# Graph attention on one Trainium2 core: P turned by VectorE blocks and transfers inside SBUF instead of by TensorE

## The chip, the core and the metric

The kernel runs on one core of a Trainium2 chip. The metric is the device time of one execution in microseconds (us). TensorE is the engine of the matrix products (PE in the rows, PEld its weight loads), VectorE is DVE, ScalarE is ACT, GpSimd is POOL, and SyncE, whose queue issues the DMAs here, is SP.

## The reference, cut to what matters

`x` is 2048x256, `adj` 2048x2048 (sparse, with many exact zeros), the projections `Wq`, `Wk`, `Wv` are 256x2048 and `Wout` is 2048x256. There are eight heads.

```python
q = (x @ Wq).reshape(h, n, d)          # h = 8, n = 2048, d = 256
k = (x @ Wk).reshape(h, n, d)
v = (x @ Wv).reshape(h, n, d)
a = einsum('hnd,hmd->hnm', q, k) * d ** -0.5
a = a + adj + adj
a = where(adj == 0, -1e6, a)
a = where(adj == 0, 0, softmax(a))
out = einsum('hnm,hmd->hnd', a, v)
out = out.transpose(1, 0, 2).reshape(n, h * d) @ Wout
result = layernorm(x + out)
```

The `reshape` is a plain one, so that head h is made from 256 rows of x only (`rows_of(x, h)`), and its 2048 rows of q, k and v are these 256 rows times eight column blocks of the weights.

## The kernel before, in words

**Tiles.** A head has 16 tiles of 128 queries, and a tile has all 2048 keys, in four banks of 512. So there are 128 tiles in all. The 16 tiles of a head are eight blocks c of two (f = 0 and 1).

**Precision by halves.** Every operand of a product is held as a high and a low part (HI and LO, both fp32r). A product is three: high by high, high by low, low by high. ScalarE writes the high part from PSUM or from a raw weight (`hi_of` L171, `hi_w` L186), VectorE or GpSimd subtracts it from the source to give the low part (`lo_of` L209, `lo_w` L196).

**One tile.** TensorE makes the scores of a bank with six matmuls of 512 columns (`scores`, L153). VectorE adds twice the mask row of that bank, held in `m_sb`, writes it to `t_p` and takes the row maximum (`score` L221, `row_max` L229). ScalarE takes the exponential of the whole 128x2048 `t_p` in place (`exp_tile` L176). Then P has to be turned, since the product with the values sums over the keys: TensorE transposes four 128x128 pieces against an identity into a PSUM bank (`turn`, L661), ScalarE and VectorE split that bank into `pt_h` and `pt_l` (L171, L209), and TensorE multiplies each 128 keys by the values, one matmul of 512 columns for the high part of P and one of 256 for the low part (`values`, L673 to L677). VectorE adds the result, over the softmax's denominator, to `y_acc` (L914, L917).

**Order on TensorE.** In `step` (L680) the four groups of a tile alternate: the transposes of group g of this tile, the scores of bank g of the next tile, the values of an earlier group. The projections of the next block and of the next head stand between them, four per block: q, k, v, and the product of v with `Wout` (Wout is applied to the values, so that the sum over heads goes straight into `y_acc`). Each is twelve matmuls of 256 columns (`project` L146). K and V of a head are thus made during the head before, and there are two copies of each in SBUF (`k0`, `k1`, `v0`, `v1`). Head 0 is made in a prologue (L360 to L507).

**The mask.** The mask row of a tile is built once from `adj` by VectorE, in four chunks (a mark L243, a put L255), during the prologue and head 0; it is stored to DRAM (`m_dram`, L301) and read back for every tile of every head in pieces of 256 KB (L304). All DMAs are issued by SP in a hand-written order, each behind the semaphore that frees its place.

**Code form.** The blocks of a head and the pairs of heads run in register loops (`heads`, L527), the last head unrolled for VectorE only. After the last head come the moments, the square root and the normalisation (L816 to L841, L519), the first 15 tiles ahead of the last.

## Time and profile before

| what | us |
|---|---|
| median of 3 runs | 2095.36 |
| lowest and highest | 2095.27, 2095.44 |
| span of the profiled execution, first to last instruction | 2092.3 |
| what lies around the span (median less span) | 3.1 |
| TensorE busy in the span | 2043.2 |
| VectorE, ScalarE, GpSimd busy | 1159.7, 843.0, 264.9 |

The profile has no device time of its own for the profiled execution beside the span, so the 3.1 us are taken from the median of the runs. The span is from the first to the last instruction on the chip. A busy time is the sum over an engine's instructions; matmuls overlap in the pipeline, so their durations are longer than their spacing, and costs on TensorE are best read as distances between starts.

### The profile page before, as it was taken

Reading aid. Unit: us, or ns where it says so; the run is one execution under the profiler, and the core shown is the slowest. Engines: PE = TensorE matmul, PEld = TensorE weight load, DVE = VectorE, ACT = ScalarE, POOL = GpSimd, SP = SyncE. Lnnn points to the kernel's source line nnn. Section 1 sums busy time; section 2 is a strip of 40 time slices with the busy share of each in tenths; the row PEclk is TensorE's granted clock in tenths of the full one; section 3 lists DMA queues with packets and bytes.
Section 4 is the critical chain, followed back from the end, with each engine's and each line's share of the span. In section 5 each row is a group of like instructions: output and inputs, shape, how many; then the busy total and the mean of one; then the engine's idle time right before and its main releaser. Section 6 shows DMA issues by size and latency. Waiting matters only on the chain.

```text
span 2092.3 us, 36481 instructions
## 1 busy us (share of the span) xinstructions
PE 2043.2 (98%) x12320; PEld 1789.0 (86%) x12320; DVE 1159.7 (55%) x2852; ACT 843.0 (40%) x1364; POOL 264.9 (13%) x207
## 2 busy tenths in 40 slices
PE   7899999999999999999999999999999999999997
PEld 7777788888888888888888888888888888888886
DVE  7788874454545445454555454455445445445555
ACT  4333333443443444334434434443344343343333
POOL 5111111101101101111011011011011111000000
PEclk9999999999999999999999999999999999999999
DMA  6766643333333333233333333333333332323332
GB/s 234 234 205 202 205 141 102 88 89 100 86 101 96 85 96 95 82 101 85 90 103 88 96 94 86 98 99 85 95 100 86 97 96 80 99 81 83 83 87 74
DMA packets 145607, 226.42 MB, mean 108 GB/s; under 512 B 12928, under 2 KB 70272, under 8 KB 143488
## 3 DMA queue, kind: packets, MB, share of 16 engines
q1 hardware_dynamic: 145536, 225.50, 36.9%
q8 instruction: 42, 0.69, 0.1%
q14 instruction: 29, 0.24, 0.0%
HBM read 206.57 MB, written 18.87 MB: 108 GB/s over the span
## 4 chain that ended last, share of the span: by engine, by line
PE 87%; DVE 5%; DMA 2%; issue 2%; ACT 0%; DVEq 0%; SPq 0%
PE bank L153 31%; PE bank L677 19%; PE bank L146 14%; PE bank L676 10%; PE bank L661 10%; DMA m_dram<-m_build 2%; DVE m_build L255 2%; PE bank L673 1%; PE bank L674 1%; DVE t_p L221 1%; DVE zero_mark L243 1%; DVE pt_l L209 0%; DVE k L209 0%; DVE y_acc L519 0%; DVE y_acc L914 0%
## 5 line engine op out<-in xcount | busy, mean ns | idle before, releaser
L153 PE MATMUL bank<-k,q_split 128*128 128x512 f32 x3072 | 840.8, 409 | 3.5 <-DVE k L209 2.5
L677 PE MATMUL bank<-v,pt_h 128*128 128x512 f32 x1856 | 673.5, 395 | 0.0
L153 PEld LDWEIGHTS bank<-k,q_split 128*128 128x128 f32 x3072 | 541.5, 190 | 95.7 <-issue 4.4
L209 DVE TENSOR_TENSOR pt_l<-bank,pt_h 128x512 fp32r<-128x512 f32 x496 | 342.7, 691 | 401.5 <-PE bank L153 392.5
L171 ACT ACTIVATE pt_h<-bank 128x512 fp32r<-128x512 f32 x496 | 296.2, 597 | 615.3 <-PE bank L661 615.2
L676 PE MATMUL bank<-v,pt_l 128*128 128x256 f32 x1856 | 522.5, 282 | 0.0
L677 PEld LDWEIGHTS bank<-v,pt_h 128*128 128x128 f32 x1856 | 348.9, 188 | 69.2
L676 PEld LDWEIGHTS bank<-v,pt_l 128*128 128x128 f32 x1856 | 350.5, 189 | 13.6
L221 DVE CUSTOM_DVE_ANT_0 t_p<-bank,m_sb 128x512 f32<-128x512 f32 x512 | 348.2, 680 | 1.8 <-PE bank L153 1.8
L176 ACT ACTIVATE t_p<-t_p,small 128x2048 f32<-128x2048 f32 x128 | 256.4, 2003 | 164.7 <-DVE small L229 157.5
L661 PE MATMUL bank<-ident,t_p 128*128 128x128 f32 x2048 | 307.6, 273 | 5.8 <-ACT t_p L176 3.7
L661 PEld LDWEIGHTS bank<-ident,t_p 128*128 128x128 f32 x2048 | 252.6, 140 | 51.2 <-ACT t_p L176 5.6
L196 POOL TENSOR_TENSOR w_q<-raw_w_q,w_q 128x512 fp32r<-128x512 f32 x63 | 81.4, 1292 | 1583.2 <-ACT w_q L186 1583.2
L914 DVE SCALAR_TENSOR_TENSOR y_acc<-bank,small,y_acc 128x256 f32 (+1 forms) x128 | 61.3, 479 | 170.3 <-PE bank L677 170.3
L209 DVE TENSOR_TENSOR k<-bank,k 128x512 fp32r<-128x512 f32 (+1 forms) x80 | 55.2, 690 | 161.3 <-ACT k L171 153.1
L171 ACT ACTIVATE vt_split<-bank 128x512 fp32r<-128x512 f32 x64 | 38.2, 597 | 221.2 <-PE bank L146 221.2
L146 PE MATMUL bank<-xt,w_k 128*128 128x256 f32 x768 | 104.3, 286 | 6.3 <-DVE k L209 6.3
L146 PEld LDWEIGHTS bank<-xt,w_k 128*128 128x128 f32 x768 | 100.9, 192 | 10.7 <-issue 7.1
L146 PE MATMUL bank<-xt,w_v 128*128 128x256 f32 x768 | 104.1, 286 | 2.3 <-DVE w_v L196 2.1
L146 PEld LDWEIGHTS bank<-xt,w_v 128*128 128x128 f32 x768 | 101.7, 193 | 5.1 <-DVE xt L209 2.5
L146 PEld LDWEIGHTS bank<-xt,w_q 128*128 128x128 f32 x768 | 100.1, 189 | 5.1
L146 PE MATMUL bank<-w_out,vt_split 128*128 128x256 f32 x768 | 102.7, 283 | 1.8 <-DVE v L209 1.8
(69 smaller groups left out, 1394.7 us busy)
## 6 DMA issues: line engine op xcount, KB each, us to landing
m_sb<-m_dram SPq DMA_DIRECT2D x508, 256.0 KB, 3.2
adj_chunk<-in_adj_dram SPq DMA_DIRECT2D x64, 256.0 KB, 3.0
raw_w_q<-in_L_gnn_Wq_dram SPq DMA_DIRECT2D x63, 256.0 KB, 3.7
raw_w_k<-in_L_gnn_Wk_dram SPq DMA_DIRECT2D x56, 256.0 KB, 3.9
raw_w_v<-in_L_gnn_Wv_dram SPq DMA_DIRECT2D x56, 256.0 KB, 4.1
m_dram<-m_build SPq DMA_DIRECT2D x14, 1024.0 KB, 5.0
raw_x<-in_x_dram SPq DMA_DIRECT2D x8, 256.0 KB, 4.4
place<-in_L_gnn_Wv_dram SPq DMA_DIRECT2D x8, 256.0 KB, 6.4
```

The lines of the kernel that those rows point to most:

```text
L146: mm = nc.tensor.matmul(dst[:, o * R:(o + 1) * R], left[:, a, k, o * P:(o + 1) * P], right[:, b, k, :], start=(i == 0), stop=(i == len(TER ...
L153: mm = nc.tensor.matmul(score_bank[b][:], q_split[:, a, k, f * P:(f + 1) * P], k_both[:, kk, k, b * BANK:(b + 1) * BANK], start=(i == 0), ...
L171: nc.scalar.activation(dst, src, ACT.Copy, scale=scale).then_inc(hi_sem, 1)
L176: nc.scalar.activation(t_p[:], t_p[:], ACT.Exp, bias=neg_max, scale=1.0, accum_out=row_sum).then_inc(exp_done, 1)
L196: eng.tensor_tensor(w_split[name][:, LO], src, w_split[name][:, HI].bitcast(F32), ALU.subtract).then_inc(w_lo[name], 1)
L209: ins = nc.vector.tensor_tensor(dst, src, hi.bitcast(F32), ALU.subtract)
L221: nc.vector.tensor_tensor_reduce(out=t_p[:, b * BANK:(b + 1) * BANK], in0=score_bank[b][:], in1=m_sb[:, b, :], scale=2.0, scalar=LOWEST, o ...
L255: nc.vector.scalar_tensor_tensor(out=m_made(v).rearrange("p (c r) -> p c r", c=C)[:, :, q * rows:(q + 1) * rows], in0=zero_mark[:].rearran ...
L661: mm = nc.tensor.transpose(pt_bank[g % 2][:, j * P:(j + 1) * P], t_p[:, (TPB * g + j) * P:(TPB * g + j + 1) * P], ident[:])
L676: nc.tensor.matmul(*lo_v, start=False, stop=False)
L677: mm = nc.tensor.matmul(*hi_v, start=False, stop=(g == BANKS - 1 and j == TPB - 1))
L914: nc.vector.scalar_tensor_tensor(out=y, in0=y_bank[:, 0:D], scalar=rdenom, in1=y, op0=ALU.mult, op1=ALU.add).then_inc(y_half, 1)
```

## The change

The kernel is rewritten around the same arithmetic. What is different:

- **P is turned off TensorE.** VectorE transposes the 128x2048 `t_p` in blocks of 32x32 with one instruction (`turn`), into one of two places `blocks`, with the blocks of one partition quarter laid side by side. Sixteen DMAs of 32 partitions by 512 elements (64 KB each) then move each quarter to its partitions in `p_turned` (`shuffle`, issued by SP). ScalarE writes the high parts of P from there in four pieces (`hi_p`), GpSimd the low parts (`lo_p`), instead of VectorE from PSUM.
- **Values run three tiles behind.** In TensorE's step tau the scores of tile tau alternate with the values of tile tau - 3 (LAG). Two places each for `p_split` and `y_bank`; the other six PSUM banks are one ring for scores and projections.
- **One K and one V.** A head's K (and first q) are projected in a burst at its tile 0, and its V and V times Wout in a burst at its tile 3. The other seven q come one in every second tile. Weights pass through five slots (SLOTS), whose low parts GpSimd makes.
- **No prologue.** The mask row of tile t + 1 is built during tile t of head 0, with two places for `adj` chunks (in the end of `y_acc`). The mask row of a tile is read back whole, 1 MB, by a DMA from ScalarE's queue, into one of two places.
- **The end.** The first 15 tiles are normalised together, after the moments of the last tile, all by VectorE.
- **No loops.** All 128 tiles are written out on every engine.

The diff, cut to its core:

```diff
+QUAD, QUADS = 32, 4
+LAG = 3
+RING = 6
+SLOTS = 5
...
-                def turn(g):
-
-                    for j in range(TPB):
-                        mm = nc.tensor.transpose(pt_bank[g % 2][:, j * P:(j + 1) * P],
-                                                 t_p[:, (TPB * g + j) * P:(TPB * g + j + 1) * P], ident[:])
-                    mm.then_inc(turned, 1)
...
+                def shuffle(tau, i):
+                    if i == 0:
+                        sp.wait_ge(turned, tau + 1)
+                    if tau:
+                        sp.wait_ge(p_lo, 4 * (tau - 1) + i + 1)
+                    for j in range(QUADS):
+                        sp.dma_start(p_turned[quad(j), i * BANK:(i + 1) * BANK],
+                                     blocks[tau % 2][quad(i), j * BANK:(j + 1) * BANK]).then_inc(shuffled[i], 16)
...
+                for tau in range(ALL + 1):
+                    h, t = divmod(tau, TILES)
+                    if h == 0:
+                        store_m(t)
...
+                    for i in range(QUADS):
+                        if opens:
+                            load_w_behind("k", h, 3 + i)
+                        if sums:
+                            load_w_behind("vt", h, 2 + i)
+                        if tau:
+                            shuffle(tau - 1, i)
+                        if h == 0 and t + 1 < TILES:
+                            load_adj((t + 1) * BANKS + i)
...
+                for tau in range(ALL + LAG):
+                    h, t = divmod(tau, TILES)
+                    if tau < ALL and t == 0:
+                        if h:
+                            wait_emptied(("x", h))
+                        for c in range(C):
+                            project_x(("k", h, c))
+                        project_x(("q", h, 0))
+                    if tau < ALL and t == VALUES_FROM:
+                        pe.wait_ge(wout_lo, h + 1)
+                        for c in range(C + 1):
+                            if c < C:
+                                project_x(("vt", h, c))
+                            if c:
+                                wait_emptied(("vt", h, c - 1))
+                                project(("v", h, c - 1), vt_split[(c - 1) % 2], w_out)
+                    for g in range(BANKS):
+                        if tau < ALL:
+                            scores(tau, g)
+                            if g == 1 and t % 2 == 0 and t <= LAST_Q:
+                                project_x(("q", h, t // 2 + 1))
+                            if g == 1 and t == TURN_X and h + 1 < H:
+                                turn_x(h + 1)
+                        if tau >= LAG:
+                            values(tau - LAG, g)
...
+                def lo_p(tau, i):
+                    hi, lo = (by_chunk(p_split[tau % 2][:, part])[:, :, i, :] for part in (HI, LO))
+                    pool.wait_ge(p_hi, 4 * tau + i + 1)
+                    nc.gpsimd.tensor_tensor(lo, p_turned[:, i * BANK:(i + 1) * BANK].rearrange(
+                        "p (j b) -> p j b", b=QUAD), hi.bitcast(F32), ALU.subtract).then_inc(p_lo, 1)
...
+                def hi_p(tau, i):
+                    if i == 0 and tau >= 2:
+                        act.wait_ge(y_done, tau - 1)
+                    act.wait_ge(shuffled[i], 64 * (tau + 1))
+                    nc.scalar.activation(by_chunk(p_split[tau % 2][:, HI])[:, :, i, :],
+                                         p_turned[:, i * BANK:(i + 1) * BANK].rearrange("p (j b) -> p j b", b=QUAD),
+                                         ACT.Copy).then_inc(p_hi, 1)
...
+                    if 1 <= tau <= ALL:
+                        exp_tile(tau - 1)
+                    if TILES <= tau + 1 < ALL:
+                        load_m(tau + 1)
+                    if tau < ALL and t == 0:
+                        for c in range(C):
+                            hi_of(("k", h, c))
+                            hi_w(w_order["k", h, c] + 4)
+                            if c % 2 == 1 and tau:
+                                hi_p(tau - 2, c // 2)
+                        hi_of(("q", h, 0))
...
+                def turn(tau):
+                    if tau >= 2:
+                        for i in range(QUADS):
+                            dve.wait_ge(shuffled[i], 64 * (tau - 1))
+                    dve.wait_ge(exp_done, tau + 1)
+                    nc.vector.transpose(blocks[tau % 2][:].rearrange("p (q j b) -> p j q b", q=QUADS, b=QUAD),
+                                        t_p[:].rearrange("p (j q b) -> p j q b", q=QUADS, b=QUAD)
+                                        ).then_inc(turned, 1)
...
+                    if tau > LAG:
+                        add_y(tau - LAG - 1)
...
+                    elif 1 <= tau <= ALL:
+                        turn(tau - 1)
+                    for b in range(BANKS):
+                        if tau < ALL:
+                            score(tau, b)
+                            if b == 0 and tau:
+                                denominator(tau - 1)
+                            if b == 2 and t % 2 == 0 and t <= LAST_Q:
+                                lo_of(("q", h, t // 2 + 1))
...
+                            if b == BANKS - 1:
+                                row_max(tau)
+                            if tau + 1 < TILES and t != VALUES_FROM:
+                                build(t + 1, b)
```

`load_w_behind(key)` issues the weight loads up to five places behind `key`, each of which waits until TensorE has used the slot it takes. `lo_w(n)` and `hi_w(n)` split all weights up to number n, in order. `build` is a mark and a put as before; `load_adj(a)` waits for the put of chunk a - 2.

## Rows read from the trace of the kernel before

**Rows 1.** The page's chain that ended last: shares of the span by line
```profile
PE bank L153 31%; PE bank L677 19%; PE bank L146 14%; PE bank L676 10%; PE bank L661 10%; DMA m_dram<-m_build 2%; DVE m_build L255 2%; PE bank L673 1%; PE bank L674 1%; DVE t_p L221 1%; DVE zero_mark L243 1%; DVE pt_l L209 0%; DVE k L209 0%; DVE y_acc L519 0%; DVE y_acc L914 0%
```

**Rows 2.** Timeline of PE in one tile: start us, us, engine, line, out<-in
```profile
1203.74 0.60 PE L661 MATMUL bank<-ident,t_p 128*128 128x128 f32 x4
1204.10 1.63 PE L153 MATMUL bank<-k,q_split 128*128 128x512 f32 x6
1205.57 0.39 PE L673 MATMUL bank<-v,pt_h 128*128 128x512 f32 x1
...
1206.98 0.38 PE L661 MATMUL bank<-ident,t_p 128*128 128x128 f32 x2
...
1212.03 1.58 PE L146 MATMUL bank<-xt,w_q 128*128 128x256 f32 x12
1213.45 0.28 PE L676 MATMUL bank<-v,pt_l 128*128 128x256 f32 x1
```

**Rows 3.** Timeline of DVE at the prologue's end, where it waits for each bank of scores
```profile
61.90 0.69 DVE L221 CUSTOM_DVE_ANT_0 t_p<-bank,m_sb 128x512 f32<-128x512 f32 x1 [0.66 <-PE bank L153]
...
63.26 0.69 DVE L221 CUSTOM_DVE_ANT_0 t_p<-bank,m_sb 128x512 f32<-128x512 f32 x1 [0.66 <-PE bank L153]
```

**Rows 4.** Timeline of ACT: the exponentials of tile 0 and of tile 16
```profile
64.74 2.00 ACT L176 ACTIVATE t_p<-t_p,small 128x2048 f32<-128x2048 f32 x1 [7.19 <-PEq L360]
...
338.07 2.01 ACT L176 ACTIVATE t_p<-t_p,small 128x2048 f32<-128x2048 f32 x1 [2.39 <-DVE small L229]
```

**Rows 5.** Groups by line over the whole span: busy us, mean ns, idle before and releaser
```profile
L221 DVE CUSTOM_DVE_ANT_0 t_p<-bank,m_sb 128x512 f32<-128x512 f32 x512 | 348.2, 680 | 1.8 <-PE bank L153 1.8
...
L171 ACT ACTIVATE pt_h<-bank 128x512 fp32r<-128x512 f32 x496 | 296.2, 597 | 615.3 <-PE bank L661 615.2
L176 ACT ACTIVATE t_p<-t_p,small 128x2048 f32<-128x2048 f32 x128 | 256.4, 2003 | 164.7 <-DVE small L229 157.5 <-PEq L360 7.2
...
L196 POOL TENSOR_TENSOR w_q<-raw_w_q,w_q 128x512 fp32r<-128x512 f32 x63 | 81.4, 1292 | 1583.2 <-ACT w_q L186 1583.2
...
L917 DVE SCALAR_TENSOR_TENSOR y_acc<-bank,small,y_acc 128x256 f32 (+1 forms) x128 | 61.9, 484 | 4.6
...
L243 DVE TENSOR_SCALAR_CACHE_REDUCE zero_mark<-adj_chunk 128x512 uint8<-128x512 f32 x64 | 43.7, 682 | 3.7 <-PEq L360 0.6
...
L519 DVE TENSOR_SCALAR y_acc<-y_acc,small,m_sb 128x256 f32<-128x256 f32 x14 | 5.2, 440 | 0.1
...
```

**Rows 6.** DMA issues: count, KB of each, median us from issue to landing
```profile
adj_chunk<-in_adj_dram SPq DMA_DIRECT2D x64, 256.0 KB, 3.0
...
raw_w_k<-in_L_gnn_Wk_dram SPq DMA_DIRECT2D x56, 256.0 KB, 3.9
...
out_dram<-y_acc SPq DMA_DIRECT2D x6, 128.0 KB, 3.0
```

**Rows 7.** Timeline of SP's queue: the time that one issue takes there
```profile
11.15 1.17 SPq L364 DMA_DIRECT2D place<-in_L_gnn_Wv_dram  x1
...
1214.38 0.38 SPq L294 DMA_DIRECT2D raw_w_q<-in_L_gnn_Wq_dram  x1
```

**Rows 8.** The page's DMA queue: packets, MB, share of 16 engines over the span
```profile
q1 hardware_dynamic: 145536, 225.50, 36.9%
```

**Rows 9.** Groups by line: the slower of GpSimd's subtractions, in the first 50 us
```profile
L196 POOL TENSOR_TENSOR w_v<-place,w_v 128x512 fp32r<-128x512 f32 x7 | 12.7, 1811 | 1.8 <-ACT w_v L186 1.8
```

**Rows 10.** Timeline of PE: the second projection of the prologue
```profile
9.70 2.76 PE L146 MATMUL bank<-xt,w_k 128*128 128x256 f32 x12
```

**Rows 11.** Line 255's puts of the mask: duration in ns, least/median/most, first and last start
```profile
L255 DVE SCALAR_TENSOR_TENSOR m_build<-zero_mark,adj_chunk x56: 1092/1189/1816, 28.4 to 283.7; 128x512 f32<-128x512 uint8 x56
```

**Rows 12.** Timeline of PE after its wait at 63 us
```profile
66.89 0.66 PE L661 MATMUL bank<-ident,t_p 128*128 128x128 f32 x4 [3.67 <-ACT t_p L176]
67.30 2.72 PE L153 MATMUL bank<-k,q_split 128*128 128x512 f32 x6
```

**Rows 13.** Window 60 to 80 us: busy of PE, PEld, DVE, ACT, POOL, then granted clock, DMA
```profile
60.00:80.00 20.00, 16.33 (x83) 13.56 (x82) 12.11 (x33) 6.75 (x11) 5.15 (x4) 0.91 0.80 243
```

1103 lines of the change are left out of this document (461 added, 642 removed).

## The prediction

> **What bounds the kernel now.** I read the chain that ended last first [rows 1]: 86 of 100 parts lie on TensorE's lines, nothing else has more than 2%, and TensorE is busy 98% of the span. VectorE, ScalarE and GpSimd have room. Of TensorE's work, line 661, the transposes of P, is 10% of the chain. What a group of it costs is read from distances between starts, not from durations [rows 2]: transposes to scores 0.36 us, scores to values 1.47, values to the next transposes 1.41, a projection 1.42. A tile has four such groups and on average two projections: 4 x 3.24 + 2 x 1.42 = 15.8 us. Tile 0's exponential starts at 64.7 and tile 16's at 338.1 [rows 4]: head 0, where masks are built, takes 17.1 a tile.
>
> **What leaves TensorE.** The 0.36 us go. So does more: where four banks of scores follow each other without transposes, VectorE, waiting for each, sees them 1.36 us apart [rows 3], not 1.47. I take 1.36, since the values ahead of a bank let its first weights load under a matmul; were it 1.47, that is 512 x 0.11 = 56 us more. A group is then 1.36 + 1.41 = 2.77, a tile without projections 11.1 us. All of TensorE: 128 x 11.08 + 256 x 1.42 = 1782 us, a floor; a head is 16 x 11.08 + 32 x 1.42 = 222.7.
>
> **What takes its place, in a tile of heads 1 to 7.** Times from E, the end of the tile's last scores.
> - VectorE scores the last bank (0.7) [rows 5] and takes the maximum (0.2), ScalarE's exponential is 2.0 + 0.2: done by 3.3 with the hand-overs. Then `turn`. The trace has no VectorE transpose. Nearest is an instruction at one element a cycle: 512 elements in 0.68 us, so 2048 in 2.1 to 2.7; a factor of two for blocks written apart, 5 us, is the other end (nothing suggests less than a cycle an element). I take 2.3. `t_p` is free at 5.6. The next bank of scores stood ready at about 2.8, the second at 5.6, the third at 8.3; six ring banks hold them, VectorE catches up by the third, and TensorE doesn't notice. This holds up to a turn of about 5 us.
> - VectorE's sum is 4 x 0.8 + 2.3 + 1.0 (adding y) + about 0.9 of small ones and q: 7.4 of 11.1.
> - SP now issues 16 more DMAs a tile. An issue takes 0.38 us in the steady part [rows 7]; at 0.4 they take 6.4, beside 0.8 for weights. Landing is 3.0 us, whether 128 or 256 KB [rows 6]; I take that for 64 KB. So the last quarter has landed at 5.6 + 6.4 + 2.6 = 14.6.
> - The copies: a high piece 0.6 on ScalarE, a low piece 1.29 on GpSimd [rows 5], which gets 4 x 1.29 a tile more (7.1 of 13.9 with weights). Four pieces after the next tile's exponential end near 11.1 + 3.3 + 0.6 + 5.2 = 20.2. Values of this tile are due at 1.4 + 2 x 11.1 + 1.4 = 25. Slack 5 us; with GpSimd's slowest mean, 1.81 [rows 9], still 3.
> - The DMA engines: 225.5 MB took 36.9% of 16 engines [rows 8], 3.4 us a MB. One MB more a tile gives (1.05 + 1.05 + 0.5) x 3.4 = 8.9 of 13.9 us. Reading masks whole moves nothing in the sum.
>
> So between bursts TensorE stays the bound: no stall.
>
> **The bursts.** At tile 0 of a head, TensorE wants nine projections in 12.8 us. ScalarE comes late (its exponential and issue of the mask end at about E + 3.9), and then has per projection a high part, a weight and half a piece of P, 1.55 us. A weight slot's round is landing 3.9 + SP 0.4 + 0.6 + 1.29 + 1.42 and waits, about 9 us for five. GpSimd: 1.29 + 0.65 = 1.94. The queues are in order and cross: SP's weight loads stand behind transfers of P that wait for `p_lo`, ScalarE's high parts behind those loads. Followed through, the ninth projection ends about 4 us late, its high and low part (1.5) are exposed before the first scores, and a load behind a transfer adds 1 to 2: 6.5 us a head. At tile 3 the spacing is 2.84 a pair, and only the first hand-over shows: 1. Heads 1 to 7: 7 x (222.7 + 7.5) = 1611.
>
> **Head 0.** No prologue and no loaded-ahead weights: the first projection needs x and a low part from GpSimd, as the second one of before, which began at 9.7 [rows 10]; I say 9. VectorE then has ten low parts and four chunks of mask, 19 us: first scores at 28, tile 0 done at 41. In every further tile VectorE has four chunks more at 0.68 + 1.19 and gaps [rows 5, 11], 2.0 each, and each `adj` load is issued by SP behind four transfers (1.6), with only two places. From the end of a turn: chunk 0 lands at 4.6, done 6.6; score, chunk 1: 9.4; score, half a q, chunk 2: 12.5; score and maximum 13.5; chunk 3 with its count 15.9; y 16.9; turn 19.2. VectorE sets the pace, not TensorE (11.8). Tiles 1 and 2: 18 each, to 77. Tile 3 with 16 projections: 32, to 109. Tiles 4 to 14: 11 x 19.2, to 320; tile 15: 10, to 330. Before, the same point was 338 [rows 4]: here all that the transposes give back is lost.
>
> **The end.** After the last scores: turn done at 5.6, issues and landing 14.6, copies 16.6, 16 value pairs 22.3, y and moments 24; then, as all 15 tiles wait for the last one, the root with its table (3), 16 x 0.44 [rows 5], and a store of 3.0 [rows 6]: about 37.
>
> **Sum.** 330 + 1611 + 37 = 1978 for the span. The profiled execution's span is 2092.3; the runs' median is 3.1 more. 1981 us.
>
> **Two rules of the Trainium skill.** The puts of the mask took 1.09 to 1.82 us [rows 11], GpSimd's subtraction 1.29 over the run [rows 5] and 1.81 on average early, when VectorE built masks [rows 9]. The Trainium skill (SBUF — State Buffer, Who interferes with whom) says that a VectorE instruction with two SBUF inputs and a GpSimd one that reads SBUF exclude each other: the trace agrees, with these spreads. GpSimd is now busy in much of head 0: if each put took 1.82, head 0 grows by 60 x 0.63 = 38 us, an upper end.
> The group's starts say that the transposes cost TensorE 0.47 us per 512 keys [rows 2, 3]. The Trainium skill (VectorE: DVE Perf Modes, Rules for kernel authors) says to use TensorE for a 128x128 transpose where PSUM will do as its place, which speaks against this change; no run of the kernel before shows the other way. It is rival 2.
>
> **Rivals.**
> 1. More stalls, still faster. A turn of 5 us costs head 0 13 x 2.7 = 35; interference in head 0 38; TensorE's clock: after a wait of 3.67 us six score matmuls took 2.72 us instead of 1.63 [rows 12], and the stretch's clock was 0.91, so partly 1.2 and not 2.4 GHz [rows 13]; such a wait at seven bursts and in 13 tiles would add 20 x 1.5 = 30. Two thirds of that: about 2050. For it: many in-order queues that cross. Against: slack of 3 to 5 us.
> 2. The transfers take over, and it is slower. Place: SP's queue, 16 issues a tile. In the busy first stretch issues took up to 1.17 us [rows 7]. It decides where a mean tile reaches (2092 - 37 - 9) / 128 = 16.0 us: (16.0 - 1.2) / 16 = 0.92 us an issue. At 1.0: 128 x 17.2 + 46 = 2248. For it: the queues' share rises to 64%, and the sixteen are small. Against: steady issues take 0.38, and these are of 32 partitions.
> By the Trainium skill (SBUF — State Buffer, The DMA setup-cost knee) a loop of 64 KB transfers runs at 138 GB/s; an estimate from it is 16 x 65.5 KB / 138 = 7.6 us a tile for the transfers alone, which with masks and weights would come close to the 13.9.
> 3. Cheaper than told: head 0's loads arrive in time (16 a tile) and the burst at tile 0 hides: 1981 - 40 - 30 = 1911.
>
> **Chances.** Forecast 0.62, rival 1 0.20, rival 2 0.12, rival 3 0.06. Of rival 1 a little may come out near no change. What a measurement tells from no change is 0.2%, 4 us: faster 0.87, same 0.01, slower 0.12. The likeliest case alone is 1940 to 2020; to hold 8 in 10 the range takes in rival 1 and the near side of rival 3: 1925 to 2070.
>
> **What would show it.** TensorE about 1800 us of work with scores 1.36 apart; transfers issued within 0.4 and landed within 3; turn 2.3; steady tiles of 11.1 or 12.5 us; tile 16's exponential near 340; waits of TensorE in each head only around tile 0, behind ScalarE or VectorE's k and q. I am wrong if SP's queue has no idle time, if TensorE waits for `p_lo` in ordinary tiles, or if head 0 is far from 330.

## The result, and the profile after

| | before | after |
|---|---|---|
| median, us | 2095.32 | 2122.34 |
| lowest to highest, us | 2092.35 to 2095.44 | 2119.43 to 2125.36 |
| runs | 4 | 4 |
| span of the profiled execution, us | 2092.3 | 2118.5 |
| ratio after / before, 95% interval | | 1.0134, 1.012 to 1.0149 |

The forecast was 1981, in a range of 1925 to 2070. The kernel is 27 us slower than before and 141 slower than the forecast. Two executions, one of the kernel with `adj` first and weights on ScalarE (5567 us) and one of the kernel before beside the last experiments (6572 us), stand so far above all others of the same kernel that they are left out as a slow state, the cause of which is not known. The parts of the page that answer to [rows 1, 5, 6, 8], with the clock, and last the chain by engine of the kernel before:

```profile
PE 1892.7 (89%) x10272; PEld 1643.0 (78%) x10272; DVE 1147.5 (54%) x2356; ACT 829.5 (39%) x1364; POOL 907.3 (43%) x718
...
PEclk9698878799999999999999999999999999999998
...
q1 hardware_dynamic: 170656, 226.64, 39.4%
...
PE 58%; SPq 9%; DMA 8%; issue 3%; DVE 2%; POOL 2%; ACT 2%; POOLq 0%; DVEq 0%; ACTq 0%
PE bank L367 23%; PE y_bank L390 14%; PE bank L339 11%; SPq L257 8%; PE y_bank L388 8%; DMA p_turned<-blocks 3%; POOL p_split L449 2%; DMA raw_w<-in_L_gnn_Wk_dram 1%; DMA raw_w<-in_L_gnn_Wv_dram 1%; DMA raw_x<-in_x_dram 1%; DVE blocks L599 
...
L449 POOL TENSOR_TENSOR p_split<-p_turned,p_split 128x512 fp32r<-128x512 f32 x512 | 652.2, 1295 | 909.4 <-ACT p_split L506 907.6
...
L599 DVE STREAM_TRANSPOSE blocks<-t_p 128x2048 f32<-128x2048 f32 x128 | 295.6, 2310 | 69.5 <-ACT t_p L497 68.3
...
p_turned<-blocks SPq DMA_DIRECT2D x2048, 64.0 KB, 2.0
...
raw_w<-in_L_gnn_Wk_dram SPq DMA_DIRECT2D x64, 256.0 KB, 4.9
...
raw_x<-in_x_dram SPq DMA_DIRECT2D x8, 256.0 KB, 4.9
```
```profile
PE 87%; DVE 5%; DMA 2%; issue 2%; ACT 0%; DVEq 0%; SPq 0%
```

TensorE is no longer busy for 98% of the span but for 89%, and of the chain only 58 parts of 100 lie on it, where before it had 87; SP's queue (SPq) has 9 and DMAs 8, where before they had 0 and 2. Yet the pieces cost what they should: the VectorE transpose, L599, takes 2.31 us (the forecast took 2.3), GpSimd's low part of P 1.295 (1.29), a 64 KB transfer lands in 2.0 (3.0). So it is the waiting that is new. Where it arises is read from the starts of the exponentials. Those of tile 0, of tile 16 and of the last tile, in ScalarE's timeline of the kernel after:

```profile
44.09 2.01 ACT L497 ACTIVATE t_p<-t_p,small 128x2048 f32<-128x2048 f32 x1 [0.59 <-DVE small L591]
...
414.83 2.01 ACT L497 ACTIVATE t_p<-t_p,small 128x2048 f32<-128x2048 f32 x1 [4.97 <-DVE small L591]
...
2079.95 2.01 ACT L497 ACTIVATE t_p<-t_p,small 128x2048 f32<-128x2048 f32 x1 [4.20 <-DVE small L591]
```

Before, these stood at 64.74, 338.07 [rows 4] and 2070.87. So the stretches compare as follows:

| stretch | before | after | difference |
|---|---|---|---|
| start to tile 0's exponential | 64.7 | 44.1 | -20.6 |
| to tile 16's (head 0) | 273.3 | 370.7 | +97.4 |
| to the last tile's (heads 1 to 7) | 1732.8 | 1665.1 | -67.7 |
| to the end | 21.4 | 38.5 | +17.1 |
| span | 2092.3 | 2118.5 | +26.2 |

The intervals between the exponentials of head 1, from the same timeline: 11.1, 12.6, **35.9**, 12.6, 11.1, 12.6, 11.1, 12.6, 11.1, 12.6, 11.1, 12.6, **18.6**, 11.1, 11.1, **35.7**. The ordinary tiles are the forecast's 11.1 and 12.5. The time that was not forecast stands at three places: the projections of V at tile 3 (a little), the turning of x at tile 13, and the burst of K at the next head's tile 0. Head 0 is `22.1 19.8 49.0 19.4 20.6 20.4 ...` and then a last interval of 44.1.

**SP's queue.** Its timeline in steady tiles, to be compared with the 0.38 of [rows 7]:

```profile
1222.97 21.14 SPq L257 DMA_DIRECT2D p_turned<-blocks  x32
1244.15 0.58 SPq L226 DMA_DIRECT2D raw_w<-in_L_gnn_Wk_dram  x1
```

32 transfers in 21.14 us are 0.66 apiece. Two tiles take 23.7 us, and of these SP issues for 21.7: the queue is 92% full, where the forecast had 6.4 + 0.8 of 13.9. And in head 0, where the queue has pauses:

```profile
197.32 0.33 SPq L249 DMA_DIRECT2D m_dram<-m_sb  x1
200.92 2.58 SPq L257 DMA_DIRECT2D p_turned<-blocks  x4
203.54 0.58 SPq L242 DMA_DIRECT2D y_acc<-in_adj_dram  x1
```

The issue after a long pause takes 0.33 (the store of the mask). In a run four transfers take 2.4 to 2.6, 0.60 to 0.65 each, and a load of 256 KB of `adj` between them 0.58. [rows 7] had shown one issue after a pause, and one of another kind. Both count. Below, the first transfer of P after a pause of over 2 us, from a window that ends behind it, and then a run of loads in the kernel before:

```profile
70.71 0.52 SPq L257 DMA_DIRECT2D p_turned<-blocks  x1
```
```profile
320.38 0.43 SPq L294 DMA_DIRECT2D raw_w_q<-in_L_gnn_Wq_dram  x1
320.86 0.47 SPq L294 DMA_DIRECT2D raw_w_k<-in_L_gnn_Wk_dram  x1
```

A load is 0.33 to 0.38 after a pause and 0.43 to 0.47 behind another load; a transfer of P is 0.52 after a pause and, with the gap behind it, 0.6 to 0.66 in a run. So a run of the loads that the kernel before had would still have given 0.5 and not 0.66.

**Who waits.** The waits of the kernel after, by engine, line and what it waited for (us in all, times, longest):

```profile
DVE zero_mark L633 <- DMA y_acc<-in_adj_dram: 85.0, 38, 7.9
...
PE y_bank L386 <- POOL p_split L449: 54.3, 11, 6.6
...
PE bank L339 <- POOL w_slot L438: 43.7, 14, 8.8
...
PE bank L352 <- DMA raw_x<-in_x_dram: 37.5, 8, 8.9
```

TensorE waits 37.5 us for the loads of x in eight turns, and 43.7 for low parts of weights. VectorE waits 85 us for `adj`. The burst at the start of head 5's K shows how the second comes about; SP's queue, then ScalarE, then TensorE:

```profile
1353.98 5.02 SPq L257 DMA_DIRECT2D p_turned<-blocks  x7
1359.04 0.58 SPq L234 DMA_DIRECT2D raw_w<-in_L_gnn_Wout_dram  x1
1359.67 1.52 SPq L226 DMA_DIRECT2D raw_w<-in_L_gnn_Wk_dram  x3
```
```profile
1358.35 0.59 ACT L491 ACTIVATE k_split<-bank 128x512 fp32r<-128x512 f32 x1
1363.33 0.63 ACT L483 ACTIVATE w_slot<-raw_w 128x512 fp32r<-128x512 f32 x1 [4.39 <-DMA raw_w<-in_L_gnn_Wk_dram]
```
```profile
1353.75 7.34 PE L339 MATMUL bank<-x_t,w_slot 128*128 128x256 f32 x60
1365.35 8.53 PE L339 MATMUL bank<-x_t,w_slot 128*128 128x256 f32 x48 [4.26 <-POOL w_slot L438]
1376.53 1.68 PE L367 MATMUL bank<-k_split,q_split 128*128 128x512 f32 x6 [2.65 <-issue]
```

TensorE goes through the projections whose weights are there, from 1353.75 on, 60 matmuls or five projections in 7.34. The slot of the first was free at about 1355.2, but SP issues transfers of P until 1359.0, then issues `Wout`, and the weight loads from 1359.67. The first lands at 1363.3, and TensorE goes on at 1365.35, after 4.26 idle. Then it is slow as well: 48 matmuls, four projections, in 8.53 us, where the ones ahead of the wait took 4 x 1.47 = 5.9: after the wait its clock is lower, 0.66 from 1365 to 1374 us against 1.00 from 1353 to 1361. In the view by stretch (us, busy of PE, PEld, DVE, ACT, POOL, then granted clock) the clock is low in head 0 too, first the kernel after, then the kernel before:

```profile
1365.00:1374.00 9.00, 8.53 (x48) 8.33 (x48) 2.93 (x5) 5.51 (x10) 7.81 (x7) 0.66 0.50 137
120.00:330.00 210.00, 153.87 (x686) 126.44 (x687) 141.27 (x293) 50.35 (x83) 59.00 (x48) 0.83 0.50 156
```
```profile
120.00:330.00 210.00, 196.54 (x1172) 168.97 (x1171) 170.57 (x387) 79.34 (x128) 23.46 (x18) 1.00 0.56 183
```

A clock of 0.83 is a mixture of 1.2 and 2.4 GHz. In head 0 TensorE is not what sets the pace, not even in the burst at tile 3: there it waits 22.7 us for low parts that VectorE makes (L567), and VectorE has the chunks of the next mask between them and waits for `adj`.

### The profile page after: what moved, and what is told of

Read it like the earlier page. It is cut to its first block, busy times and chain, and to the rows that moved or that the text cites. A ratio compares the mean times of both kernels' runs of the same rounds, so it can differ in the third digit from the quotient of the medians.

```text
span 2118.5 us, 29153 instructions
## 1 busy us (share of the span) xinstructions
PE 1892.7 (89%) x10272; PEld 1643.0 (78%) x10272; DVE 1147.5 (54%) x2356; ACT 829.5 (39%) x1364; POOL 907.3 (43%) x718
## 3 DMA queue, kind: packets, MB, share of 16 engines
q1 hardware_dynamic: 170656, 226.64, 39.4%
## 4 chain that ended last, share of the span: by engine, by line
PE 58%; SPq 9%; DMA 8%; issue 3%; DVE 2%; POOL 2%; ACT 2%; POOLq 0%; DVEq 0%; ACTq 0%
PE bank L367 23%; PE y_bank L390 14%; PE bank L339 11%; SPq L257 8%; PE y_bank L388 8%; DMA p_turned<-blocks 3%; POOL p_split L449 2%; DMA raw_w<-in_L_gnn_Wk_dram 1%; DMA raw_w<-in_L_gnn_Wv_dram 1%; DMA raw_x<-in_x_dram 1%; DVE blocks L599 1%; PE y_bank L386 1%; ACT p_split L506 1%; POOL w_slot L438 0%; PE bank L352 0%
## 5 line engine op out<-in xcount | busy, mean ns | idle before, releaser
L449 POOL TENSOR_TENSOR p_split<-p_turned,p_split 128x512 fp32r<-128x512 f32 x512 | 652.2, 1295 | 909.4 <-ACT p_split L506 907.6
L367 PE MATMUL bank<-k_split,q_split 128*128 128x512 f32 x3072 | 808.3, 400 | 32.6 <-issue 23.1
L390 PE MATMUL y_bank<-v_split,p_split 128*128 128x512 f32 x1920 | 718.8, 406 | 0.0
L367 PEld LDWEIGHTS bank<-k_split,q_split 128*128 128x128 f32 x3072 | 591.5, 193 | 150.6 <-issue 24.5
L388 PE MATMUL y_bank<-v_split,p_split 128*128 128x256 f32 x2048 | 566.0, 287 | 0.0
L390 PEld LDWEIGHTS y_bank<-v_split,p_split 128*128 128x128 f32 x1920 | 371.8, 194 | 80.9
L388 PEld LDWEIGHTS y_bank<-v_split,p_split 128*128 128x128 f32 x2048 | 400.3, 195 | 23.5
L506 ACT ACTIVATE p_split<-p_turned 128x512 fp32r<-128x512 f32 x512 | 298.4, 621 | 281.9 <-DMA p_turned<-blocks 275.6
L339 PE MATMUL bank<-x_t,w_slot 128*128 128x256 f32 x2304 | 324.5, 298 | 55.7 <-POOL w_slot L438 43.7
L339 PEld LDWEIGHTS bank<-x_t,w_slot 128*128 128x128 f32 x2304 | 314.5, 206 | 65.3 <-POOL w_slot L438 44.1
L599 DVE STREAM_TRANSPOSE blocks<-t_p 128x2048 f32<-128x2048 f32 x128 | 295.6, 2310 | 69.5 <-ACT t_p L497 68.3
L339 PEld LDWEIGHTS bank<-w_out,vt_split 128*128 128x128 f32 x768 | 99.0, 196 | 36.1 <-DVE vt_split L567 36.1
L386 PE MATMUL y_bank<-v_split,p_split 128*128 128x512 f32 x128 | 55.2, 431 | 54.3 <-POOL p_split L449 54.3
L567 DVE TENSOR_TENSOR k_split<-bank,k_split 128x512 fp32r<-128x512 f32 x64 | 43.9, 688 | 90.4 <-ACT k_split L491 90.4
L567 DVE TENSOR_TENSOR v_split<-bank,v_split 128x512 fp32r<-128x512 f32 x64 | 44.3, 692 | 78.6 <-ACT v_split L491 78.6
```

The source lines that it names most:

```text
L339: mm = nc.tensor.matmul(dst[:, o * R:(o + 1) * R], left[:, a, k, o * P:(o + 1) * P], right[:, b, k, :], start=(i == 0), stop=(i == len(TER ...
L367: mm = nc.tensor.matmul(dst[:], q[:, a, k, f * P:(f + 1) * P], k_split[:, kk, k, b * BANK:(b + 1) * BANK], start=(i == 0), stop=(i == len( ...
L388: nc.tensor.matmul(y[:, 0:D], lo, v_split[:, j, HI], start=False, stop=False)
L390: mm = nc.tensor.matmul(y[:], hi, v_split[:, j].rearrange("p s d -> p (s d)"), start=False, stop=last)
L449: nc.gpsimd.tensor_tensor(lo, p_turned[:, i * BANK:(i + 1) * BANK].rearrange("p (j b) -> p j b", b=QUAD), hi.bitcast(F32), ALU.subtract).t ...
L506: nc.scalar.activation(by_chunk(p_split[tau % 2][:, HI])[:, :, i, :], p_turned[:, i * BANK:(i + 1) * BANK].rearrange("p (j b) -> p j b", b ...
```

## The experiments

The theory after this result, called A in the expectations: SP's queue, with issues of 0.6 and not 0.4 us, is nearly full; it does not slow the ordinary tile, but everything else that SP issues (weights, x, `adj`) is late behind it. The rival: what is late is late for other reasons (ScalarE's and GpSimd's work, landing, engines), or the gain on TensorE is not what was reckoned. Each time below is a median of 3 to 5 runs, with the ratio to the kernel before on the same chip. Two are single runs, read for their traces. The kernel after was not run beside them, and the kernel before took 2092 to 2093 us there and not 2095: differences to the kernel after are good to about 3 us. "Head" is the distance from one head's first exponential to the next one's, heads 1 to 6.

**Adj first.** SP issues the load of `adj` ahead of the four transfers of that quarter.

```diff
+                        if h == 0 and t + 1 < TILES:
+                            load_adj((t + 1) * BANKS + i)
                         if tau:
                             shuffle(tau - 1, i)
-                        if h == 0 and t + 1 < TILES:
-                            load_adj((t + 1) * BANKS + i)
```

> SP issues each adj load ahead of the four transfers of P of the same i, not behind them; nothing else changes. Theory A (SP's queue: an issue of a transfer takes 0.60 us there, so four of them delay the load behind them by 2.4 us, and VectorE waits for the chunk): head 0's tiles go from 20.4 to about 18.1 us, tile 16's exponential from 414.8 to about 385, the whole to about 2092. Theory B (VectorE's own work, 4 scores, 4 chunks, turn and y, with TensorE's wait for the low parts of P, sets head 0): tiles stay within 0.5 us of 20.4 and the whole within 8 us of 2122.

Measured: 2075.65, ratio 0.9922 (0.9899 to 0.9944), 47 us below the kernel after. Its waits:

```profile
DVE zero_mark L633 <- DMA y_acc<-in_adj_dram: 36.2, 38, 7.0
```

The wait for `adj` fell from 85.0 to 36.2 us, the ordinary tiles of head 0 from 20.4 to between 16.6 and 18.7, tile 3 from 49.0 to 40.2, tile 16's exponential came at 370.0 instead of 414.8, and nothing else changed. Four issues ahead of each of its four loads cost a tile 2.5 to 3 us. A holds; the gain was larger than its numbers.

**Weights, x and Wout from ScalarE's queue.** ScalarE issues each load when it takes the high part of the projection that frees the slot.

```diff
                 def hi_of(key):
                     hi_only(key)
+                    n = w_order[key] + SLOTS if key in w_order else len(w_keys)
+                    if n < len(w_keys):
...
+                        act.dma_start(raw_slot[n % SLOTS][:], columns).then_inc(w_loaded[n % SLOTS], 16)
+                    if key[0] == "q" and key[2] == C - 1 and key[1] + 1 < H:
+                        act.dma_start(raw_x[:], rows_of(x, key[1] + 1)).then_inc(x_loaded, 16)
```

> All weight, x and Wout loads after the first five are issued by ScalarE right behind the high part of the projection that frees their place; SP keeps the transfers of P and the adj loads. Theory A (loads stand on SP behind transfers issued at 0.60 us each): the interval between the exponentials of tiles 15 and 16 of a head goes from 36.5 to about 31 us, that of tiles 12 to 13 from 18.1 to 12 to 13, a head from 244 to about 232, the whole to about 2035. Theory B (ScalarE's and GpSimd's chain per projection, 1.55 and 1.94 us, makes the burst late, whoever issues): burst interval stays above 35, a head loses at most the 6 us of x; the issues on ScalarE (0.33 to 0.6 us each) may make the burst longer.

Measured: 2032.17, ratio 0.9712 (0.9696 to 0.9728), 90 us below the kernel after. A head is 231.2 to 232.9 instead of 243.2 to 245.5: 18.6 at tile 13 became 11.6, the burst at tile 0 31 to 33 instead of 36.5, tile 3 35.0 instead of 36. The DMA issues of its page (KB of each, median us from issue to landing), and two of its waits:

```profile
raw_w<-in_L_gnn_Wk_dram ACTq DMA_DIRECT2D x59, 256.0 KB, 3.7
```
```profile
DVE zero_mark L625 <- DMA y_acc<-in_adj_dram: 81.5, 32, 7.9
...
PE bank L330 <- DMA raw_x<-in_x_dram: 3.7, 1, 3.7
```

Loads of `Wk` land in 3.7 instead of 4.9, and the wait for x is 3.7 us in one turn (the first) instead of 37.5 in eight. `adj` waits as before (81.5), since that part was not touched.

**x turned a tile later** (`TURN_X = LAST_Q + 2`), on the kernel after alone.

> The x of the next head is turned by TensorE in tile 14 and not in tile 13; all else as in the changed kernel. If TensorE's 4 to 9 us wait for raw x in tile 13 is a loss of its own: every head but the last gets 6 to 7 us shorter (tile 12 to 13 at 11.1), the whole 40 to 50 us less, about 2077. Rival: the time lost there is only shifted (the burst at tile 0 waits for weights that come late anyway, and VectorE's low part of x comes nearer to it): less than 15 us.

Measured: 2073.46, ratio 0.9919 (0.9892 to 0.9946), 49 us below. TensorE's wait for x fell from 37.5 to 3.7 us in all, the interval at tile 13 to 11.1 (and that of tile 14 to 11.6, the four transposes of x being 0.5). So this term is 6.5 us a head, and it comes from one load that was asked for too late.

**Every transfer in two**, of 32 KB, so that SP has 32 issues a tile and the bytes stay.

```diff
-                        sp.dma_start(p_turned[quad(j), i * BANK:(i + 1) * BANK],
-                                     blocks[tau % 2][quad(i), j * BANK:(j + 1) * BANK]).then_inc(shuffled[i], 16)
+                        for e in range(2):
+                            half = BANK // 2
...
```

> Each transfer of P (32 partitions x 512 elements) is issued as two of 256 elements: 32 issues a tile for the same bytes. Theory A (price per issue, 0.60 us whatever the size): SP needs 19.5 us a tile and becomes the bound, steady tiles go from 11.1 and 12.6 to about 20.5, the whole to about 2900. Rival (price by bytes or by descriptors' size, SP has room): an issue takes about 0.3 and steady tiles stay under 13, the whole under 2200.

Measured, a single run: 3220.95. A head is 377 to 380, a mean of 23.6 a tile, where A had 20.5 and 2900 for the whole. SP's queue and its place in the chain:

```profile
1222.73 47.39 SPq L259 DMA_DIRECT2D p_turned<-blocks  x73
```
```profile
q1 hardware_dynamic: 268960, 226.77, 25.0%
...
SPq L259 58%; PE bank L342 4%; DMA p_turned<-blocks 3%; PE bank L370 3%; PE y_bank L393 1%; POOL p_split L452 1%; DVE blocks L602 1%; DMA raw_w<-in_L_gnn_Wk_dram 1%; PE y_bank L391 1%; DMA raw_w<-in_L_gnn_Wv_dram 1%; DMA raw_w<-in_L_gnn_Wq_
...
p_turned<-blocks SPq DMA_DIRECT2D x4096, 32.0 KB, 1.9
```

73 issues in 47.39 us are again 0.65 each, for half the bytes. 32 x 0.65 = 20.8, with the other loads 22; what the remaining 1.6 us are, the run does not say. The DMA engines are not the limit: q1's share fell from 39.4 to 25.0% of the longer span (805 against 835 us). Now rival 2 of the prediction is there in full, with SP's line 58 parts of the chain. It also shows that the price of an issue does not depend on its bytes.

**Adj first and weights on ScalarE together.**

> The edits of e1_adj_first and e2_weights_on_act together. Theory A says that both take away delays behind the same queue at different places (head 0; the bursts and the load of x), so the gains add: 2122 - 47 - 90 = about 1985 us, tile 16's exponential near 350 and heads at 232. Rival: with the weights on ScalarE the queue of SP is no longer late in head 0 either, so that part of the gains is the same one: 2005 to 2030.

Measured: 1986.08, ratio 0.9485 (0.9467 to 0.9503); 136 us below the kernel after, and the two alone gave 47 + 90 = 137. The terms are separate. Tile 16's exponential comes at 355.1, a head is 230.7 to 233.9.

**Values two tiles behind** (`LAG = 2`), on the kernel after.

> LAG = 2 in place of 3: values two tiles behind; V is projected at tile 2; all else as in the changed kernel. My working had 5 us to spare at three behind, with the low parts of P ready 20.2 us after the end of their tile's scores and wanted at 25. Then at two behind they are wanted at 14 and TensorE waits about 6 us in every tile: steady tiles go from 11.1 and 12.6 to 17 to 19, the whole to about 2122 + 700 = 2800. Rival (the chain from the turn to the low parts is shorter than counted, three behind buys nothing): tiles stay under 13.

Measured, a single run: 2939.89. Ordinary tiles take 19.5 and 21.4 us; TensorE now waits for the low parts of P in nearly every tile:

```profile
PE y_bank L386 <- POOL p_split L449: 725.3, 120, 11.3
```

With three tiles of distance it was 54.3 us in 11 waits, none of them between tile 16's exponential and the last one. A wait is 6.0 us on average, as expected, but a tile grew by 8.4 to 8.8, and the clock from 600 to 1000 us is 0.85 instead of 0.97. The third tile is what hides the whole way of P through VectorE, SP, ScalarE and GpSimd, as the step on slack said; but what of the 5 us was left, this run does not say.

**The early normalisation**, on adj first and weights on ScalarE: VectorE normalises the first 15 tiles while it waits for the last one's values.

```diff
+                    if tau == ALL + LAG:
+                        all_vars(0, slice(0, TILES - 1))
+                        inverse_std(0, slice(0, TILES - 1))
+                        normalise(0, TILES - 1)
...
-                inverse_std(0, slice(0, TILES - 1))
-                normalise(0, TILES - 1)
```

> e5_adj_and_weights with the first 15 tiles normalised while the last tile's values are still being waited for. My working of the end has 15 x 0.44 plus the root's steps, about 9 us, behind the last y. If these are all that is exposed there: the last exponential to the end goes from 38.5 to about 29, the whole 9 us under e5. Rival: what follows the last exponential is set by the transfers, the copies and the store, and less than 4 us are gained.

Measured: 1978.98, ratio 0.9453 (0.9439 to 0.9466), 7 us less where 9 were expected. From the last exponential to the end it takes 31.9 instead of 39.7 us.

**A quarter of the transfers from ScalarE's queue**, added to that.

```diff
-                        if tau:
+                        if tau and i < QUADS - 1:
                             shuffle(tau - 1, i)
...
+                    if 1 <= tau <= ALL:
+                        shuffle_last(tau - 1)
```

> e7_and_early_norm with the last four of the sixteen transfers of a tile issued from ScalarE's queue, behind its high parts of P: 12 issues on SP, 4 on ScalarE. Theory A (SP's issues are what is late): with 2.4 us less per tile on SP, head 0's tiles get 1 to 2 us shorter (the adj loads stand behind fewer issues), and the last exponential to the end 1 to 2; steady tiles stay 11.1 and 12.6: 15 to 25 us under e7. Rival: ScalarE, which now waits for the low parts of P before it can issue, delays the next exponential or the high part of q; the whole stays the same or grows.

Measured: 1978.86, ratio 0.9456 (0.9443 to 0.9469): nothing, a miss for A. Heads are 230.5 to 234, head 0 is 320 instead of 315.6. From the last exponential to the end it takes 29.8 instead of 31.9, as A had it, but ordinary tiles of head 0 are no shorter, and ScalarE's exponentials now stand behind its own issues and their waits, the rival's point (last line below; this wait was not there before). So the run shows that the move pays nothing; what SP's queue alone would have given back it doesn't separate. On ScalarE's queue an issue of this kind costs the same, 0.65:

```profile
1307.32 2.60 ACTq L512 DMA_DIRECT2D p_turned<-blocks  x4
...
1311.59 0.39 ACTq L475 DMA_DIRECT2D raw_w<-in_L_gnn_Wv_dram  x1
```
```profile
ACT t_p L489 <- issue: 62.9, 12, 6.9
```

A weight load after a pause takes 0.39 there.

**Two transposes of four left out**, in the kernel before. In this run half of P is not turned: two of a group's four 128x128 pieces keep what stood in the bank. The copies and values are made as before.

```diff
-                    for j in range(TPB):
+                    for j in range(TPB // 2):
```

> The kernel before, with two of a group's four transposes on TensorE left out (the other half of each bank of turned P holds old data, so half of P is not P); the splits, values and waits stay. The working of the prediction has a group at 3.24 us with its four transposes and 2.77 without, 0.47 for four. If TensorE is the bound and its price is per transpose, half of them is 512 x 0.235 = 120 us: about 1975. Rival (the pace of a group is set by the chain from the exponential over the splits, or by weight loads that a shorter group exposes): less than 60 us gained.

Measured: 1992.89, ratio 0.9527 (0.9511 to 0.9543), 100 us less for 1024 transposes: 0.098 apiece, and if the other half is worth the same, 200 us for all. Reckoned had been 512 x 0.47 = 241 and for half of them 120. In ordinary tiles of heads 1 to 6 the gain is 0.9 us (14.7 to 13.8, 16.9 to 16.0), and 4 x 0.235 = 0.94 was reckoned; in head 0 it is only 0.3 a tile. So most of the gain was there to be had. TensorE's timeline, to be compared with [rows 2]:

```profile
1203.65 0.38 PE L661 MATMUL bank<-ident,t_p 128*128 128x128 f32 x2
1203.79 1.63 PE L153 MATMUL bank<-k,q_split 128*128 128x512 f32 x6
```

From the transposes to the scores it is 0.14 instead of 0.36.

**The first k ahead of the exponential**, on the early normalisation: ScalarE takes the high part of the burst's first projection, and issues the load behind it, before the exponential.

```diff
+                    early = 0 < tau < ALL and t == 0
+                    if early:
+                        hi_of(("k", h, 0))
                     if 1 <= tau <= ALL:
                         exp_tile(tau - 1)
```

> e7_and_early_norm, and at a head's first tile ScalarE takes the high part of the first K block, and issues the weight load behind it, ahead of the exponential of the tile before, not behind it. If what is left of the burst (32 us between the exponentials of tiles 15 and 16, 25.3 by TensorE's work alone) is the round of the five weight slots, started late by the exponential: that interval goes to 30 or below, 7 x 2 = 14 us less than e7. Rival (ScalarE's work per projection sets the burst, and the exponential now comes later itself): no change, or up to 10 us more.

Measured: 1978.65, ratio 0.9457 (0.9441 to 0.9472): nothing. The two intervals at the burst were 11.1 + 31.5 = 42.6 and are 13.4 + 29.4 = 42.8: only the exponential between them moved, by 2.3 us. The edit's premise does not hold. In the kernel with the early normalisation ScalarE's queue issues the load while the exponential is still running:

```profile
1251.95 2.01 ACT L489 ACTIVATE t_p<-t_p,small 128x2048 f32<-128x2048 f32 x1 [3.88 <-DVE small L583]
1253.42 0.41 ACTq L475 DMA_DIRECT2D raw_w<-in_L_gnn_Wk_dram  x1
```

Counted from the start of TensorE's burst, the first three loads are issued after 1.6, 3.1 and 4.5 us, each when a projection is done, in heads 2 to 7 of both kernels (here 1253.42 less 1251.77, with the edit 1251.12 less 1249.47). So no load was issued sooner, and the "2.3 us earlier" of the last expectation below is not so either. What the loads do wait for, the DMA view of the burst shows, in the kernel with the early normalisation (KB of each, median us from issue to landing):

```profile
m_sb<-m_dram ACTq DMA_DIRECT2D x1, 1024.0 KB, 6.0
...
raw_w<-in_L_gnn_Wk_dram ACTq DMA_DIRECT2D x3, 256.0 KB, 6.4
```

Over the whole run the same loads land in 3.8 us; here it is 6.4, for ScalarE has issued the 1 MB of the next mask just ahead of them, on the same queue.

**The mask behind the burst**, once on the early normalisation, once on the one above as well.

```diff
-                    if TILES <= tau + 1 < ALL:
+                    if TILES <= tau + 1 < ALL and t:
                         load_m(tau + 1)
...
                         hi_wout(h)
+                        if TILES <= tau + 1 < ALL:
+                            load_m(tau + 1)
```

> This is the kernel with adj first, weights from ScalarE's queue and the early normalisation; the one edit more is that at the first tile of a head ScalarE issues the 1 MB load of the next mask behind the nine high parts of the burst instead of ahead of them. Theory A: the burst at tile 0 waits because its weight loads stand behind that megabyte on the same queue (they took 6.4 us to land in the burst, 3.8 over the whole run, and TensorE waited 2.7 and 0.8 us for low parts of weights). Then the loads land in about 3.8, the 2.7 go, the interval around tile 0 falls from 31.5 to about 29, a head from 231.2 to 228.5, and the time by 7 x 2.7 = 19 us, to about 1960. Theory B: the pace of the burst is that of GpSimd and ScalarE, 1.94 us for a weight and half a piece of P against 1.42 on TensorE; then the loads land sooner and a head loses less than 1 us, about 1974 to 1979.

> Both edits together: ScalarE takes the high part of the first k ahead of the exponential (alone it gave nothing, since the loads that it issued 2.3 us earlier still landed 5.6 to 7 us later), and the megabyte of mask goes behind the burst. Theory A: the earlier loads are now worth something, a head falls by 2.7 + 2.3 = 5 us less the 2.3 that the exponential comes later, to between 226.5 and 228.5, about 1945 to 1960. Theory B: no change against the kernel with the mask moved alone, or a loss of up to 2.3 a head.

Measured: 1960.2, ratio 0.9367 (0.9354 to 0.9381), and 1967.07, ratio 0.9398 (0.9385 to 0.9411). The first is A's number. The DMA view of its burst, and TensorE's timeline there in both kernels, first the one with the early normalisation:

```profile
raw_w<-in_L_gnn_Wk_dram ACTq DMA_DIRECT2D x3, 256.0 KB, 3.6
```
```profile
1251.77 7.36 PE L317 MATMUL bank<-x_t,w_slot 128*128 128x256 f32 x60
1261.87 3.14 PE L317 MATMUL bank<-x_t,w_slot 128*128 128x256 f32 x24 [2.73 <-POOL w_slot L416]
```
```profile
1240.52 7.36 PE L317 MATMUL bank<-x_t,w_slot 128*128 128x256 f32 x60
1248.65 3.13 PE L317 MATMUL bank<-x_t,w_slot 128*128 128x256 f32 x24 [0.77 <-POOL w_slot L416]
```

The loads land in 3.6, and the wait of 2.73 us is 0.77. An interval at the burst is 29.2, a head 229.0. Whether it is the order on the queue that held the loads back, or the DMA engines that the megabyte kept busy, the two kernels do not tell apart: the transfers of P, from SP's queue, landed faster as well in this window, in 3.0 instead of 4.4. With the first k ahead of the exponential the head is 230.2. The loads are issued no sooner there either; TensorE waits after four projections (0.9 us) and not after five, since the fifth weight's high part stands behind the later exponential, and the burst ends 1.2 us later. A's number for the second, at or below the first, was missed, and B's loss is what came, at half its size.

## Why the prediction was wrong

Against its own sum, counted from the exponentials of tile 15 of head 0 and of the last tile; the last column is the kernel with `adj` first and weights on ScalarE:

| term | forecast | measured | with both edits |
|---|---|---|---|
| to the end of head 0 | 330 | 370.7 | 319.4 |
| heads 1 to 7 | 1611 | 1709.3 | 1625.2 |
| the end | 37 | 38.5 | 39.7 |
| span | 1978 | 2118.5 | 1984.3 |

Two edits of the order of issues give back 136 of the 141 us, so the cause lies there. That this kernel then stands so near the forecast is in part luck: head 0 is 11 us below its term and the rest 17 above.

- **The step that failed is the price of an issue.** "An issue takes 0.38 us in the steady part", and "at 0.4 they take 6.4". That row was one load after a pause. A transfer of P takes 0.52 after a pause, and in a long run each holds the queue for 0.66 us, so 16 take 10.6 of a tile's 11.1 us. The ordinary tile still stood at 11.1, since 0.66 is below the 0.92 at which rival 2 would have decided. Rival 2 named the right place, SP's queue, and the wrong mechanism: not the transfers were late, but all that was issued behind them.
- **Heads 1 to 7, +98.** Weights behind transfers: the burst at tile 0 takes 36.5 on average instead of the 30.4 of the sum (11.1 + 9 x 1.42 + 6.5), and 44.1 for head 1's; tile 3 36.1 instead of 34.8. 6 x 6.1 + 13.7 + 7 x 1.3 = 59. The step "a load behind a transfer adds 1 to 2" should have had 5 (36.5 against the 31.8 with the loads off SP's queue). With SP free of them the 7.5 us of bursts a head are 9.0 (231.7 against 222.7), and 6.5 with the mask behind the burst: the rest of that step was near, without a term for the megabyte of mask, which is worth 2.5. Not all of the 59 are waits, for the clock falls behind them.
- **The load of x was not in the sum at all:** 6 heads x 7.0 = 42 us, 4.1 of the 7.0 a wait, 0.5 the turning itself, and the rest, as far as is known, the lower clock behind it (0.72 from 585 to 595 us). SP asks for it behind 16 transfers of that tile, and TensorE wants it a tile later. The prediction read the burst's loads one by one and left out this one.
- **Head 0, +41.** The step had `adj` behind four transfers, at 1.6 us; they take 2.6, and there are four such loads in a tile, each wanted by VectorE at once: 20.4 instead of 19.2 in the ordinary tiles, 22.1 and 19.8 instead of 18 and 18, and tile 3 with its burst, the largest piece, 49.0 instead of 32 (40.2 with `adj` first alone). There the sum left out that mask chunks stand between the low parts of the burst in VectorE's order, for which TensorE waits 22.7 us; no run moved them. With `adj` first head 0 is 312 to 326 from tile 0 to tile 16, its ordinary tiles 17 to 18. "Tile 16's exponential near 340" did not follow from the sum even so: by it the burst comes in between, and it is 360. Likewise "the same point was 338" compares tile 15 with tile 16: before, tile 15's exponential stood at 320.6, so that the sum itself had head 0 behind by 9 us.
- **Right were:** the gain on TensorE (ordinary tiles 11.1 and 12.6, borne out by the half transposes at 100 for 120), the turn of 2.3, GpSimd's 1.29, the three tiles of distance (from tile 16's exponential to the last one TensorE never waits for low parts of P; nine of the eleven waits are in head 0), and the end within 3 us. The landing was better than taken, 2.0 for 3.0.
- **The two rules.** VectorE's puts of the mask took 1.08 to 1.76 us in the kernel after, with a median of 1.18 that is that of before [rows 11]; 64 of them at their mean of 1.20 instead of 1.08 are 8 us at most. GpSimd's low parts of P took 1.25 to 1.33 in all of the run, those of weights 1.39 on average from 100 to 300 us against 1.305 over the run. So the two engines cost each other a few us in head 0, not 38. That is the exclusion of the Trainium skill (SBUF — State Buffer, Who interferes with whom): the trace shows it small here. The Trainium skill's rule to transpose on TensorE (VectorE: DVE Perf Modes, Rules for kernel authors) had the right sign for the change as it was made, 27 us slower, but the last kernel turns P without TensorE and is 132 us faster than before, so the rule is not borne out here. And the 7.6 us a tile estimated from the Trainium skill for 64 KB transfers (SBUF — State Buffer, The DMA setup-cost knee) were not the bound; 16 issues at 0.66 came ahead of them.
- **Why slower than before, then?** Without a prologue tile 0's exponential came 21 us sooner (24 in the sum). In heads 1 to 7 the change gave 68 us, where the sum had 152 (1733 less 1611 - 30). In head 0, where masks bind VectorE and `adj` stands behind transfers, it lost 97, where the sum had 46, and 17 at the end. The chance of 0.12 for slower was too low for a queue whose price for these transfers no row showed.

The kernel with all four edits (`adj` first, weights on ScalarE, the early normalisation, the mask behind the burst) takes 1960.2 us, 6.3% below the kernel before and 7.6% below the changed one. None of the four touches the arithmetic; all four move only where in a queue something stands. What stays open is head 0, still 313 us against 273 before, where VectorE has masks, low parts and turns, and where the clock from 120 to 330 us is 0.88.

## What to carry to other kernels

Price a queue by a run of issues one behind another, and of the kind that it will get: here one load after a pause took 0.38 us, a transfer of the new kind 0.52 after a pause and 0.66 in a run, and a queue that looked half empty was 92% full. If the trace has no such issue, the price is open, and the range has to say so. When many small transfers come onto a queue, list everything else that it issues, with the time at which each is wanted, for it is these loads that turn late and not the transfers. A large load that nobody needs yet should not be issued just ahead of small urgent ones. Before moving an issue ahead of a computation on the same engine, look whether it waits for it at all.

## What the runs showed of the hardware

- The time of an issue depends on what went before and on its kind: loads and stores 0.33 to 0.42 us after a pause, loads 0.43 to 0.47 behind another load and 0.58 behind a transfer of P; transfers of 32 partitions inside SBUF 0.52 after a pause and 0.6 to 0.66 in a run, for 64 KB as for 32, and 0.65 on ScalarE's queue as on SP's. In the first microseconds single loads took up to 1.17 [rows 7]. What makes the difference between the kinds was not tried.
- ScalarE's queue issues a load while an instruction of ScalarE runs: at 1253.42 us, in the exponential from 1251.95 to 1253.96.
- 64 KB from 32 partitions to 32 others inside SBUF landed 2.0 us after the issue (median of 2048), 32 KB in 1.9.
- 256 KB loads behind 1 MB on the same queue landed in 6.4 us instead of 3.6. The Trainium skill (SBUF — State Buffer, "Can I just issue two DMAs to hit both halves?") says that each issuing engine has by default one set of rings, first in, first out, and that all DMAs run on the same 16 engines. The runs fit either as the cause and do not tell them apart: 64 KB transfers of the other queue landed in 4.4 instead of 3.0 in the same windows.
- VectorE turned 128x2048 fp32 in 32x32 blocks, written a row apart, in 2.31 us, 3.4 times the 0.69 that its instructions of 512 elements take. No run wrote the blocks side by side, so what their distance costs, if anything, is not shown.
- A wait of 4.3 us on TensorE cost more than itself: the four projections behind it took 8.5 us instead of 5.9, at a granted clock of 0.66 instead of 1.00.
